# Softmax sums in an attention kernel: inverses taken in pieces on all partitions instead of by way of DRAM, accumulating transfers placed at even distances, sum passes one pair of key tiles later

## What is computed

```python
xn = layernorm(x)
q, k, v = heads(xn @ q_w.T + q_b) / sqrt(32), heads(xn @ k_w.T + k_b), heads(xn @ v_w.T + v_b)
attn = softmax(q @ k.T)                      # per head, 2048 x 2048
ctx  = merge(attn @ v)
out  = x + (ctx @ out_w.T + out_b) + tanh(((xn @ weight) @ aux_weight1) @ aux_weight2 + bias)
```

## Time and profile before

| | us |
|---|---|
| runs, lowest / median / highest of 3 | 4203.73 / 4214.44 / 4216.61 |
| profiled execution | 4198.09 |
| its span (first to last instruction) | 4196.3 |
| TensorE matmul busy | 4120.6 (98%) |
| GpSimd busy | 3191.1 (76%) |
| VectorE busy | 2932.6 (70%) |
| ScalarE busy | 2358.5 (56%) |

### The profile page before, as it was taken

How to read it: one execution, slowest core, us unless ns; L and a number is a source line. 1 busy time by engine, 2 the same in 40 slices (tenths; PEclk the granted TensorE clock), 3 DMA queues, 4 the chain that set the end, 5 groups by cost and what they waited for, 6 DMA issues and landing times.

```text
span 4196.3 us, 77492 instructions
## 1 busy us (share of the span) xinstructions
PE 4120.6 (98%) x21728; PEld 2520.6 (60%) x21728; DVE 2932.6 (70%) x4928; ACT 2358.5 (56%) x4517; POOL 3191.1 (76%) x1119
## 2 busy tenths in 40 slices
PE   8999999899999999999999999999999999999989
PEld 6888888655555555555555555555555555555467
DVE  4343334587878878888888887878888888787434
ACT  2221222166666666666666666666666666666621
POOL 1222222289999999999999999999999999999820
PEclk9999999999999999999999999999999999999999
DMA  4444445367777777777777777767777777777677
GB/s 168 160 163 157 150 160 176 130 132 152 157 152 158 157 155 161 157 160 152 156 156 159 155 156 156 159 148 161 154 157 159 157 160 156 153 156 152 154 242 256
DMA packets 268271, 673.36 MB, mean 160 GB/s; under 512 B 109056, under 2 KB 110080, under 8 KB 214656
## 3 DMA queue, kind: packets, MB, share of 16 engines
q0 software_dynamic: 46080, 335.56, 41.9%
q1 hardware_dynamic: 138784, 220.26, 16.0%
q10 hardware_dynamic: 83040, 113.01, 9.6%
HBM read 195.30 MB, written 137.36 MB: 79 GB/s over the span
## 4 chain that ended last, share of the span: by engine, by line
PE 62%; DMA 6%; issue 5%; POOL 4%; ACT 3%; DVE 0%; ACTq 0%; POOLq 0%; SPq 0%; DVEq 0%
PE pv_bank L928 19%; PE st_bank L922 19%; PE sm_bank L906 19%; POOL pool_sum L709 4%; DMA q_stack<-max_row 3%; DMA dma_sum<-probs 3%; ACT probs L763 3%; PE sm_bank L234 2%; PE sm_bank L928 2%; PE st_bank L234 1%; PE sm_bank L915 0%; DMA q_stack<-s_ctx 0%; POOL k_stack L698 0%; DVE max_row L825 0%; ACTq L762 0%
## 5 line engine op out<-in xcount | busy, mean ns | idle before, releaser
L841 DVE TENSOR_REDUCE part_max<-sm_bank 128x1 f32<-128x512 f32 x4032 | 2461.9, 682 | 559.5 <-PE sm_bank L906 559.3
L709 POOL TENSOR_TENSOR pool_sum<-pool_sum,probs 128x2048 f32<-128x2048 f32 x512 | 2462.1, 4809 | 21.4 <-ACT probs L763 5.5
L763 ACT ACTIVATE probs<-st_bank 128x512 f32<-128x512 f32 x3840 | 1957.6, 616 | 597.9 <-PE st_bank L922 555.9
L922 PE MATMUL st_bank<-q_stack,k_stack 97*128 97x512 f32 x4096 | 1649.6, 404 | 30.2 <-DMA q_stack<-max_row 15.9
L906 PE MATMUL sm_bank<-k_stack,q_stack 96*128 96x512 f32 x4032 | 1650.6, 410 | 1.9 <-issue 1.5
L906 PEld LDWEIGHTS sm_bank<-k_stack,q_stack 96*128 96x128 f32 x4032 | 766.9, 190 | 514.4 <-DVE part_max L841 316.4
L922 PEld LDWEIGHTS st_bank<-q_stack,k_stack 97*128 97x128 f32 x4096 | 777.5, 190 | 314.9 <-ACT probs L763 137.0
L928 PE MATMUL pv_bank<-probs,v_pair 128*32 128x512 f32 x7680 | 935.4, 602 | 0.0
L928 PEld LDWEIGHTS pv_bank<-probs,v_pair 128*32 128x32 f32 x7680 | 204.6, 109 | 454.9 <-ACT probs L763 258.2
L720 POOL DMA_DIRECT2D dma_sum<-probs x320 | 300.1, 938 | 140.2 <-DMA dma_sum<-probs 132.9
L348 POOL TENSOR_TENSOR y_out<-y_out,x_in 128x512 f32<-128x512 f32 x64 | 82.7, 1292 | 386.1 <-ACT y_out L377 380.7
(11 more groups left out here) (101 smaller groups left out, 2206.4 us busy)
## 6 DMA issues: line engine op xcount, KB each, us to landing
dma_sum<-probs POOLq DMA_DIRECT2D x320, 1024.0 KB, 8.5
q_stack<-s_q_hi ACTq DMA_DIRECT2D x122, 256.0 KB, 6.2
k_stack<-s_k_hi ACTq DMA_DIRECT2D x122, 256.0 KB, 5.0
x_in<-in_x SPq DMA_DIRECT2D x16, 1024.0 KB, 7.7
s_q_hi<-qk_hi SPq DMA_DIRECT2D x16, 1024.0 KB, 4.3
s_q_lo<-qk_lo SPq DMA_DIRECT2D x16, 1024.0 KB, 6.5
s_k_hi<-qk_hi SPq DMA_DIRECT2D x16, 1024.0 KB, 4.3
s_k_lo<-qk_lo SPq DMA_DIRECT2D x16, 1024.0 KB, 6.4
```

What stands on the lines that cost most here:

```text
L709: nc.gpsimd.tensor_tensor(total[:], one[:], tile_at(r, kt)[:], ALU.add).then_inc(pool_added, 1)
L763: nc.scalar.activation(tile_at(r, kt)[:, q * BLK:(q + 1) * BLK], st_bank[:, st_place(kt * QB + q)], ACT.Exp, scale=SCALE).then_inc(probs_r ...
L841: nc.vector.tensor_reduce(part_max[:, k:k + 1], sm_bank[:, sm_place(k)], AX.X, ALU.max).then_inc(max_scores_read, 1)
L922: nc.tensor.matmul(st_bank[:, st_place(u)], k_st[r][0:ROWS + 1, kt * P:(kt + 1) * P], q_st[r][0:ROWS + 1, q * BLK:(q + 1) * BLK], start=Tr ...
```

## The change

- `spread_ratios` goes, with its tensors in DRAM, its tiles `sums_col` and `ratio_col` and its semaphores. VectorE's `recip` now takes the reciprocal of the copied sums, which stand on all 128 partitions (32 times the same row for each block of queries), in four pieces of 128 columns, straight into `ratio`. `RECIPS = [55, 63, 7, 15]` says behind which block's reduction each piece stands. The first piece waits for the copied sums and for the scaling of the head before. VectorE's body of a head now begins with block 16 (`rest`) and ends with block 15 of the next (`begin`).
- GpSimd: join 1 goes ahead of add 0, the other four behind adds 1, 3, 5 and 7. Each join now waits for the probabilities of its own tile as well. The scaling waits for the four pieces, and it goes ahead of add 8.
- `CUT` is 8 instead of 6 and `SUM_UNIT` 48 instead of 40: `add_up` and `copy_sums` come after key tile 7. The loads after tiles 6 and 7 are written in the other half of ScalarE's body, at the same places in its order.
- `heads` can hand out a second form of the next head's number, from a register that is one higher; TensorE uses it for its row maxima (`to_turn`). The value is the same.

```diff
-SUM_UNIT = 40
-RECIP_UNIT = 56
-CUT = 6
+BEGIN = 16
+SUM_UNIT = 48
+RECIPS = [55, 63, 7, 15]
+CUT = 8
...
-JOIN_AFTER = {0: (0, 1), 2: (0, 2), 4: (0, 3), 6: (0, 4), 7: (0, 5)}
+JOIN_FIRST = (0, 1)
+JOIN_AFTER = {1: (0, 2), 3: (0, 3), 5: (0, 4), 7: (0, 5)}
...
-SCALE_ADD = 7
+SCALE_ADD = 8
...
-                spread_ratios(h, r)
...
             def join(h, r, c, j):
+                pool.wait_ge(probs_ready, PRIME + h * UNITS + QB * (CHAINS[c][j] + 1))
                 if j == 1:
                     pool.wait_ge(tile_used, PRIME + h * KT + CHAINS[c][0] + 1)
...
             def scale(h, r):
                 pool.wait_ge(pv_copied, PRIME + h + 1)
-                pool.wait_ge(ratio_loaded, h * (QB * DMA) + QB * DMA)
+                pool.wait_ge(recip_ready, h * len(RECIPS) + len(RECIPS))
...
             def sum_up(h, r, i):
+                if i == 0:
+                    join(h, r, *JOIN_FIRST)
                 add(h, r, i)
...
-            def recip(h):
-                dve.wait_ge(sums_loaded, h * DMA + DMA)
-                nc.vector.reciprocal(ratio_col[:], sums_col[:]).then_inc(recip_ready, 1)
+            def recip(h, r, piece):
+                if piece == 0:
+                    dve.wait_ge(sums_copied, PRIME + h + 1)
+                    dve.wait_ge(context_ready, PRIME + h)
+                cut = [BLK // len(RECIPS) // 8 * 8 * i for i in range(len(RECIPS))] + [BLK]
+                columns = slice(cut[piece], cut[piece + 1])
+                nc.vector.reciprocal(ratio[:, columns], sum_copy[r % 2][:, columns]).then_inc(recip_ready, 1)
+
+            def maxima(s, k, units, sums_of):
+                if units:
+                    if k == 0:
+                        dve.wait_ge(row_max_ready, PRIME + s)
+                    dve.wait_ge(max_scores_ready, s * UNITS + k + 1)
+                    nc.vector.tensor_reduce(part_max[:, k:k + 1], sm_bank[:, sm_place(k)], AX.X,
+                                            ALU.max).then_inc(max_scores_read, 1)
+                if k in RECIPS and sums_of is not None:
+                    recip(*sums_of, RECIPS.index(k))
+
+            def begin(s, units=True, new=True, sums_of=None):
+                for k in range(BEGIN):
+                    if k == TURN_UNIT and new:
+                        negate(s - 1)
+                    maxima(s, k, units, sums_of)
+
+            def rest(s, units=True, sums_of=None):
+                for k in range(BEGIN, UNITS):
+                    maxima(s, k, units, sums_of)
...
-                    recip(h)
+                    for piece in range(len(RECIPS)):
+                        recip(h, r, piece)
                     low(2, 0)
                     results(1, 1)
                 else:
-                    maxima(following + 1, units=more >= 2)
+                    rest(following + 1, units=more >= 2, sums_of=(h, r))
+                    begin(following + 2, units=more >= 3, new=more >= 2, sums_of=(h, r))
```

More of the change, by code:

```diff
@@ L538, in build_attend @@
         sum_copy = [sb(f"sum_copy{s}", [P, BLK]) for s in range(2)]
-        sums_col, ratio_col, ratio = sb("sums_col", [P, PACK]), sb("ratio_col", [P, PACK]), sb("ratio", [P, BLK])
+        ratio = sb("ratio", [P, BLK])
         ctx_out = [sb(f"ctx_out{s}", [P, BLK]) for s in range(2)]
@@ L571, in build_attend, with heads @@
         CTX_DMAS = QB
-        def heads(eng, body):
+        def heads(eng, body, extra=0):
             with nc.Fori(0, ALL_HEADS // GROUP - 1, engines=[eng.engine], hint_back_edge=True,
                          head_slot={eng.engine: 0}) as i:
-                after = eng.snap(i + 1)
+                after = [eng.snap(i + 1 + n) for n in range(1 + extra)]
                 for r in range(GROUP):
-                    body(i * GROUP + r, r, GROUP, after * GROUP + (r + 1 - GROUP))
+                    body(i * GROUP + r, r, GROUP, *(a * GROUP + (r + 1 - GROUP - n * GROUP) for n, a in enumerate(after)))
             for r in range(GROUP):
-                body(ALL_HEADS - GROUP + r, r, GROUP - 1 - r, ALL_HEADS - GROUP + r + 1)
+                body(ALL_HEADS - GROUP + r, r, GROUP - 1 - r, *[ALL_HEADS - GROUP + r + 1] * (1 + extra))
         def block_pairs(eng, body):
@@ L608, in load_row @@
                 sp.dma_start(q_st[r][MROW:MROW + 1, :].bitcast(F32), max_row[:].bitcast(F32)).then_inc(row_loaded[r], DMA)
[L610 to L623, removed]
             def store(h, r):
@@ L791, in load @@
                     load_v(act, dram, h - 1, v_sb[r // 2], v_loaded[r // 2])
+            for kt in range(CUT):
+                exps(0, 0, kt)
+                if kt in LOAD_AT:
+                    load(GROUP - 1, GROUP - 1, LOAD_AT.index(kt))
             def body(h, r, more, following):
@@ L802, in body @@
                             copy_pv(h, r)
+                        if kt in LOAD_AT and more >= GROUP:
+                            load(h + GROUP, r, LOAD_AT.index(kt))
                         if kt == CUT - 1:
@@ L850, in _ @@
             negate(0)
-            maxima(1, old=False, new=False)
+            begin(1, new=False)
+            rest(1)
+            begin(2)
             def low(n, par):
@@ L987, in body @@
                     for p in range(CUT // 2):
-                        both_scores(following, r1, 2 * p, following + 1, more - 1)
-                        both_scores(following, r1, 2 * p + 1, following + 1, more - 1)
+                        both_scores(following, r1, 2 * p, to_turn + 1, more - 1)
+                        both_scores(following, r1, 2 * p + 1, to_turn + 1, more - 1)
                         if p == 0:
@@ L1008, in output @@
                                  lambda c: wo_lo[:, c]).then_inc(bank_ready, 1)
-            heads(pe, body)
+            heads(pe, body, extra=1)
             pe.wait_ge(w_loaded, 2 * DMA)
@@ L1025, in build_program @@
     dram |= {n: scratch(f"s_{n}", [DIM, DIM]) for n in ("wo_hi", "wo_lo")}
-    dram |= {n: scratch(f"s_{n}", [2, SEQ]) for n in ("sums", "ratio")}
     with ExitStack() as outer, ExitStack() as ctx:
```

20 lines of the change are left out of this document (3 added, 17 removed).

## The result

| | runs | us, lowest / median / highest |
|---|---|---|
| before | 5 | 4203.73 / 4208.46 / 4216.61 |
| after | 5 | 4178.50 / 4181.46 / 4299.33 |

In four of its five runs the changed kernel is faster: their ratio to the kernel before is 0.9931 (95% interval 0.9918 to 0.9943), and the medians are 27 us apart. The fifth took 4299.33 us. That ratio leaves such runs out, since a run this far above the others counts as disturbed; the experiments show that this one belongs to the kernel. The profiled execution is one of the short ones: 4181.14 us, span 4179.3 us, against 4198.09 and 4196.3.

A forecast was written before the change was run, and what follows sets the result against it. TensorE was taken to follow GpSimd's round, coupled through the late row of maxima. Round -12, TensorE's head start -4 and the end -3 gave -19 us from 4214.4, rounded to 4196; main case 4175 to 4225, whole range 4165 to 4310.

The forecast's parts named there:

- GpSimd's round of 49.1 us: GpSimd's joins, adds and scaling per head: 49.1 us, 0.2 below today, over 60 heads -12 us.
- a small gain: Whole kernel, main case: same GpSimd round with small gain, own range 4175 to 4225 us, chance 0.50.
- TensorE's own pace throughout: Rival, pitch of the heads: if join 5 lands within 7.5 us, pitch 48.8, -34 us, 4180; chance 0.13.
- The wait moves and does not go: GpSimd's joins: the wait between joins 4 and 5 moves to between join 5 and the next join 1.
- The row gets caught behind join 4: Rival: row of maxima issued behind join 4 lands with it, pitch 50.8, +93 us, about 4304; chance 0.31.
- The room of 5.4 us: Row of maxima ahead of TensorE's score matmuls: it may take 5.4 us to land without cost.
- A landing near 5.5 us: Sign of the main case: the row of maxima's landing stays near 5.5 us.
- A piece of 0.92 us: VectorE's reciprocal of 128 columns: 0.92 us a piece, cost 0 while under 1.1 us.
- The cover of 1.1 us a pair: VectorE's idle time while TensorE applies the probabilities: 1.1 us for each pair of key tiles, covering a piece.
- The way through DRAM: 0: Removing SP's ratio copies through DRAM: perhaps some tenths on join 3, taken as 0.
- late sum passes: 0: TensorE's sum matmuls after tile 7, not 5: last join and add get 5.8 us more, gain 0.
- The end, 3 us gained: After the last sums: copy to scaling 10 us shorter, 3 us of it counted as gain.

The follow-up runs named there:

- small v: Kernel after, with the loop's v loads fetching one key tile of 16 and one full load added ahead of the loop: median 4279.53 us.
- row first: Kernel after, with join 4 made to wait until VectorE has negated the next head's row maxima: median 4180.91 us, ratio 0.9942 to the kernel before.
- old joins: Kernel after, with the joins in the old order and the scaling ahead of add 7; pieces and late sum passes kept: median 4201.96 us, ratio 0.9998.
- row late: Kernel after, with one more 512-byte transfer that SP sends and waits for ahead of each row of maxima: median 4518.09 us.
- one piece: Kernel after with join 4 behind the negation, and the reciprocal of all 512 columns in one instruction at unit 55: median 4378.75 us.
- ScalarE's loop end: Kernel after with join 4 behind the negation, and ScalarE's loop over the heads closed two key tiles later: median 4181.89 us.
- sums back: Kernel after with join 4 behind the negation, sum passes back at unit 40 and loops closed at key tile 6: median 4179.04 us, ratio 0.9947.

## Why the prediction was right, and where it was not

4196 us was forecast, faster, and 4181.46 came, faster. Part of this is luck: the median of the first five runs is a short run, that of the next six is 4286.53 us, slower than before. For the short way the side was right; two of the terms were mis-sized, and they hid each other.

*GpSimd's round of 49.1 us* was 0.2 too long, and its case, a small gain, given half of the chance, did not come in one run. The prediction had 30.66 for the three gaps from join 1 to join 4, from a gap of 10.47 behind join 1 that belonged to the old order. In the new order that gap is 10.10, and the three are 30.33. For the gap from join 5 to join 1 it had 8.30, and 8.43 came. So the round is 48.86, and GpSimd's lag never grew to where join 3 delays the row: the row goes 8.4 us behind join 3, not 5.3 as before. The pitch came down to TensorE's own (48.8 forecast for that, 48.84 measured) and the middle gave 25.1 us where the prediction had counted 12 and 4. The pitch is that of the rival "TensorE's own pace throughout", given 0.13. But its condition, join 5 landing within 7.5 us, and its sign, GpSimd waiting for ScalarE, did not come: join 5 lands in 7.8 us on the mean, in 8.4 in the heads with a v load and in 7.2 in the others, and join 1 waits for it. That the round and TensorE's pitch are equal may come from the transfers: in the heads with a v load join 5 lands sooner the later GpSimd is against TensorE (9.6 to 7.5 us, correlation -0.8 over 29 heads). No run tests this.

*The wait moves and does not go* was right. GpSimd's idle time ahead of its joins went from 128.3 to 105.1 us and stands ahead of join 1. Join 3, for one, lands in 8.2 us on the mean instead of 9.9: with the copies through DRAM gone and nothing else it is 9.4, with the new places alone 9.2. What makes the rest of the difference stays open.

*The row gets caught behind join 4*, given 0.31, is, as far as shown, what the other runs are: five of eleven. Its numbers held well. From 1 us behind the join on, a landing of 6.4 to 8 us, self-holding: in the run with small v it was 6.45 on the mean (5.7 to 7.9 from 1 us on, and it decides from 0.4 us on), with GpSimd held at join 1 by TensorE's first tile, as written. No long run of the kernel after was profiled, so that its long runs are this state rests on the row first, which removes them, on their granted clock, and on their time: forecast 4304, measured 4282 to 4300. The prediction called it near a coin's edge, and it is. What the prediction did not see is that one program takes both ways. It forecast one time where there are two, 4180 and 4290, that lie towards its range's two ends, and it gave most chance to what lies between.

*The room of 5.4 us* for the row was right: 5.5 measured from the end of the negation to the first score matmul. A landing near 5.5 us, which the prediction named as a sign of its case, did not come: it is 2.6.

*A piece of 0.92 us* took 0.94, and it is free. Reciprocals in pieces do not change the time. The page that the prediction weighed (the Trainium skill, VectorE: DVE Perf Modes, "First, the fixed hardware budget") gave an estimated 1.2 us. From 0.940 at 128 and 3.340 at 512 columns the slope is 6.25 ns a column, where a repeat of 8 at its 0.96 GHz would be an estimated 8.3; the measurement decides. The cover of 1.1 us a pair is right in so far as 0.94 us is hidden.

*The way through DRAM: 0, late sum passes: 0* both held for the pace (ratios 0.9998). In head 61 the late sum passes go with a loss: of the kernels with them and ScalarE's loop closed at the same place, four profiles (after, twice; old joins; row first) have it at 54.6 to 56.0 us, and three (row late, small v, one piece) are at most 2 us above their own pitch there; those with the old cut lose nothing.

*The end, 3 us gained* was wrong: 11.9 lost. So -16 and -3 were forecast and about -29 and +12 came: -19 against -17.0 between the two profiled executions. The rest of the distance from 4196 to 4181 is the base, since the three runs shown of the kernel before had a median of 4214.4 and later ones 4202 to 4208. 6.9 of it are head 61. Another 4.0 lie between the last score matmul and the first matmul of the output (15.2 us against 11.2), where a scaling stands behind join 5, and 2.8 in the output's blocks (11.2 against 10.9 us each), less 1.8 elsewhere. That the end is longer goes with the new places of the joins: from the last score matmul to the end it is 196.9 to 199.4 us in the four profiles with the old places and 202.0 to 209.8 in the ten with the new ones; the two whose last score matmul comes earliest (ScalarE's loop end, sums back) have 21.5 and 20.3 us ahead of the output's first matmul. What in it costs the time was read in the trace and not tested.

## What to carry to other kernels

A small transfer that another engine waits for has to be ordered against the large ones, not timed against them: here a lead of 0.6 to 2.9 us held in six runs of eleven, and one wait on the producer's semaphore made it hold in all. When runs of one program fall into two groups, look for a place where two queues race before calling the long group a disturbance; a loop that holds itself makes two levels out of one. Where an engine's round is nearly as long as that of the bound, look at where its transfers stand: here their places and their order against the row were the whole gain, while removed copies and moved passes brought nothing. And where a wait has several conditions, compare the time at which each was met before believing the one that is named.

## What the runs showed that I had not expected

- Short stalls of TensorE cost more than their length. After it had run dry for 1.3 to 4.4 us the granted clock often, not always, went from 1.00 to 0.50, and matmuls took 0.63 us instead of 0.40; that adds about 1.65 us. In the kernel with the row late the first pair of key tiles takes over 7.2 us, by the median 7.44, in 52 of 58 heads, and not 5.79. In the run with small v, with stalls of 1.1 us on the mean, that is so in 8 of 58.
- 512 bytes took 6.7 us behind a join, and the kernel that moves 480 KB less every second head, with 15 us more in head 0, is 98 us slower than the short runs of the kernel after.
- Where a loop ends can decide on 5 us of an engine's time some ten key tiles behind it.
- The profile put 67.3 us of waits down to ScalarE that were waits for GpSimd's own transfers.
